# Reordering TensorE's step in a graph-attention kernel: projections put between the weighings

## The chip, the cores and the metric

The kernel runs on one core of a Trainium2 chip. The metric is the device time of one execution in microseconds (us). Engines are named as in the profile: PE is TensorE, PEld its loading of the stationary operand, DVE is VectorE, ACT is ScalarE, POOL is GpSimd, SP is the engine that issues the DMAs.

## The reference

The kernel computes a residual block around one graph-attention layer, for x of shape (8, 1024, 64) and an integer matrix adj of shape (8, 1024, 1024) that is 1 in about 1 of 128 places and 0 elsewhere. There are 8 heads of 64 columns.

```
h = max(layernorm(x), 0)
q, k, v = h@Wq+bq, h@Wk+bk, h@Wv+bv              # split into 8 heads
s = leaky_relu(q.k/8 + edge_bias[adj], 0.2)      # s is -1e9 where adj == 0
out = softmax(s) @ v                             # per head
result = x + (out as 512 columns) @ Wp + bp
```

## The kernel before

Rows are taken in groups of 16 query rows times 8 heads, which fill 128 partitions. Since few keys are set in adj for 16 rows, each group gathers at most 32 keys out of every 128 by a product with a matrix of zeros and ones (onehot), 256 slots for all 1024 keys. A tile is 128 rows, 8 groups; a pair is two groups; so a graph is 8 tiles or 32 pairs, and the kernel has 64 tiles or 256 pairs. Keys and values are never projected: the scores are taken against the gathered normed rows, and what is weighed is projected afterwards, head by head, with the products of Wv and Wp (w_ext).

All engines run the same count of steps s, one per pair, and each has its own function step(b, s) that issues what is due, in the order in which it is written there. Constants give the lag of each stage (line 43 to 45): a stage with lag L works on pair s - L, and a stage that is due once a tile has its work in every fourth step. Nothing else orders the work; engines meet in semaphores. Steps are told apart here by s modulo 4, as step 0, 1, 2 and 3. One graph is 32 steps; after a ramp of 32 steps the main loop has a body of 64 steps (two graphs) that is run three times, and the last two graphs are written out.

What TensorE does in a step, with the letters used further on, and its line:

- S, scores (L1174, L1175): four products with 256 columns streamed, into row_bank. Waits for VectorE's take of the scores before.
- T, turn_y (L1185): four transposes of the masked scores w, into turned_bank. Waits for VectorE's Y of the step before.
- W, weigh (L1232): four fp32 products of the exponentials pt with the gathered rows nat_sb. In the records each fp32 product is two loads and two matmuls, so eight of each.
- G and M, gather_keys (L1197) and gather_masks (L1209): two products each.
- N, natural (L1220): four products that turn the gathered keys back.
- A, turn_adj (L1240): eight bf16 transposes of adj, in step 1. C, count (L1248): eight small products, in step 2. P, project (L1263): four fp32 products (one head each, eight loads and eight matmuls), half a tile's heads in step 3 (lag 27) and the other half in step 0 (lag 28). These three share the PSUM bank adj_bank, and each waits until the one before has been read: P's by VectorE's norm, A's by ScalarE's copy_adj, C's by VectorE's take_counts.
- R, rank (L1255), in step 0; the making of the queries, Q (L1322), in steps 1 and 3; and four rarer products (L1308, L1331, L1339). They share q_bank (the program's misc) in the same way.

Before the change a step's order on TensorE is S T W G M N A C P R and then the rest of q_bank. ScalarE follows in that order: exp (L1456), copy_o (L1464), copy_keys (L1447), copy_masks (L1438), copy_natural (L1473), copy_adj (L1430), and the queries' high parts (L1483).

VectorE's order is Y (L1701, the leaky relu of two groups), take_counts (L1629), take_scores (L1678, two groups), flag_used (L1637), norm (L1762 to L1777: one half of a tile's heads is divided by its sums; the first half, e = 0, also has L1764 and L1773, and waits until GpSimd has summed the tile before), low_q (L1652, two instructions), take_ranks (L1645), small work on the row maxima (L1735, L1742, L1752), mark (L1690, onehot), pick_beta (L1662, L1666).

GpSimd's is line (L1039, two), convert (L1016, step 0, it makes adj_bf), add_heads (L1027 three times and L1030: it sums a tile's heads and adds x), and the adding of a constant to x_res twice a graph.

Of the kernel before, what the change touches and what calls it, by code (L numbers as in the profile page):

```python
# [20 lines left out]
def preln_graph_attention(nc, x, adj, Wq, bq, Wk, bk, Wv, bv, edge_bias, Wp, bp, out):  # L21
# [4 lines left out]
    B, M, D = x.shape  # L26
# [15 lines left out]

    LOAD, CONV, TURN_A, COUNT, USED, RANK, VAL, ONEHOT = 0, 4, 5, 6, 7, 8, 9, 9
    MASK, MASK_OUT, TFILL, QFILL, BETA, COLSUM, VEC = 10, 14, 13, 9, 6, 18, 22
    SCORE, A_LINE, Y, TURN, PV, X_ADD, PROJ, NORM, SUM, OUT = 17, 19, 20, 21, 22, 24, 27, 28, 30, 31
    K0, SETTLED = 32, 24
# [6 lines left out]
    with ExitStack() as ctx, ExitStack() as prep, ExitStack() as fast:  # L53
# [230 lines left out]
        def tile(b, s, lag):  # L284
            return every(b, s, lag, 4)
# [794 lines left out]
        def _(pe):  # L1080
# [44 lines left out]
            def adj_bank_uses(b, s):  # L1125
                t = tile(b, s, TURN_A)
                if t is not None:
                    yield adj_copied, TPG * b + t + 1
                t = tile(b, s, COUNT)
                if t is not None:  # L1130
                    yield cnt_ready, TPG * b + t + 1
                due = piece(b, s, PROJ, 2)
                if due is not None:
                    yield proj_taken, 2 * (TPG * b + due[0]) + due[1] + 1
# [88 lines left out]

            def weigh(b, p):
                n, t = PPG * b + p, p // 4
                pe.wait_ge(probs_ready, n + 1)
                pe.wait_ge(nat_copied, n + 1)
                if later(n):
                    pe.wait_ge(o_copied, n)
                for u in range(2):  # L1230
                    for k in range(2):
                        last = pe.matmul(o_part[0:D + 1, P * u:P * u + P], nat_sb[:, t % 2, p % 4 * 2 + u, k, :],  # L1232
                                         pt[:, p % 2, u, k, :], start=(k == 0), stop=(k == 1))
                last.then_inc(pv_done, 1)

# [21 lines left out]

            def project(b, t, e, s):
                n = TPG * b + t
                pe.wait_ge(o_copied, 4 * n + 4)  # L1260
                free(adj_bank_uses, b, s, len(list(adj_bank_uses(b, s))) - 1)
                for h in range(4):
                    last = pe.matmul(adj_bank[:, (D + 1) * h:(D + 1) * h + D + 1], ot_sb[0:D + 1, t % 2, 4 * e + h, :],  # L1263
                                     w_ext[0:D + 1, 4 * e + h, :], start=True, stop=True)
                last.then_inc(proj_done, 1)

            def step(b, s):
                p = pair(b, s, SCORE)
                if p is not None:
                    scores(b, p)  # L1270
                p = pair(b, s, TURN)
                if p is not None:
                    turn_y(b, p)
                p = pair(b, s, PV)
                if p is not None:
                    weigh(b, p)
                due = piece(b, s, TFILL, 4)
# [6 lines left out]
                if p is not None:  # L1284
                    natural(b, p)
                t = tile(b, s, TURN_A)
                if t is not None:
                    turn_adj(b, t, s)
                t = tile(b, s, COUNT)
                if t is not None:  # L1290
                    count(b, t, s)
                due = piece(b, s, PROJ, 2)
                if due is not None:
                    project(b, *due, s)
                i = 0
# [69 lines left out]
        def _(act):  # L1365
# [121 lines left out]
            def step(b, s):  # L1487
                p = pair(b, s, TURN)
                if p is not None:
                    exp(b, p)  # L1490
                p = pair(b, s, PV)
                if p is not None:
                    copy_o(b, p)
                due = piece(b, s, TFILL, 4)
                if due is not None:
                    copy_keys(b, *due)
                due = piece(b, s, MASK, 4)
                if due is not None:
                    copy_masks(b, *due)
                p = pair(b, s, SCORE)  # L1500
                if p is not None:
                    copy_natural(b, p)
                t = tile(b, s, TURN_A)
                if t is not None:
                    copy_adj(b, t)
                due = q_piece(b, s, QFILL)
                if due is not None:
                    high_q(b, *due)
                g = every(b, s, COLSUM, PPG)
                if g is not None:  # L1510
                    act.wait_ge(col_sums, b + g + 1)
                    nc.scalar.activation(mean_rep[:, :], misc[:, 0:1].to_broadcast([P, P]), ACT.Copy, scale=1.0 / M)\
                        .then_inc(mean_ready, 1)
                g = every(b, s, VEC, PPG)
                if g is not None:
                    act.wait_ge(vec_done, b + g + 1)
                    nc.scalar.activation(vecs[:, bass.ds(D * (b + g), D)], misc[:, 0:D], ACT.Copy).then_inc(vec_ready, 1)
# [30 lines left out]
        def _(dve):  # L1548
# [109 lines left out]
            def pick_beta(b, g, half):  # L1658
# [4 lines left out]
                                               head_rows[:, :], same_q[:, :].unsqueeze(1).to_broadcast([P, CAP, GQ]),  # L1663
                                               ALU.add, ALU.mult).then_inc(beta_picked, 1)
                dve.wait_ge(beta_picked, 2 * n + half + 1)
                nc.vector.tensor_reduce(beta[:, bass.ds(2 * PPG * b + 2 * PPG * g + CAP * half, CAP)],  # L1666
# [28 lines left out]
            def step(b, s):  # L1695
# [8 lines left out]
                if t is not None:  # L1704
                    take_counts(b, t)
                p = pair(b, s, SCORE)
                if p is not None:
# [3 lines left out]
                if t is not None:  # L1711
                    flag_used(b, t)
                    if t % TPG == TPG - 1:

                        dve.wait_ge(adj_copied, TPG * b + t + 1)
                        cols = square_sums_adj[:, bass.ds(TPG * b + t - TPG + 1, TPG)]
                        nc.vector.tensor_tensor(cols, cols, cnt_sums[:, :], ALU.subtract).then_inc(kinds_noted, 1)
                due = piece(b, s, NORM, 2)
                if due is not None:
                    norm(b, *due)  # L1720
                due = q_piece(b, s, QFILL + 1)
                if due is not None:
                    low_q(b, *due)
                t = tile(b, s, VAL)
                if t is not None:
                    take_ranks(b, t)
                four = p is not None and p % 2 == 1
# [12 lines left out]
                if four:  # L1740
                    dve.wait_ge(neg_ready, n + 1)
                    nc.vector.scalar_tensor_tensor(shift[:, cols], wmax[:, cols], -1.0, shift_neg[:, cols],  # L1742
                                                   ALU.mult, ALU.min).then_inc(shift_ready, 1)
                if t is not None and t % TPG == TPG - 1:
                    dve.wait_ge(val_ready, TPG * b + t + 1)
                    nc.vector.tensor_tensor(val_top[:, :], val_top[:, :], val_max[:, :], ALU.max).then_inc(vals_noted, 1)
                due = beta_piece(b, s, BETA + 1)
                if due is not None:
                    pick_beta(b, *due)
                if four:  # L1750
# [106 lines left out]
```

## Time and profile before

| | |
|---|---|
| time, median of 3 runs | 1049.67 us (1048.76 to 1053.98) |
| the profiled execution's own time | 1053.46 us |
| its span, first to last instruction | 1051.7 us |
| PE, PEld busy | 989.4 us (94%), 974.2 us (93%) |
| DVE busy | 917.3 us (87%) |
| ACT, POOL busy | 779.8 us (74%), 493.6 us (47%) |
| mean granted TensorE clock | 0.985 |

A record's duration on PE contains the pipeline's depth, so durations of neighbours overlap; the time from one start to the next tells what an instruction costs there. The same holds for DVE: neighbours overlap by some 0.08 us.

### The profile page before, as it was taken

How to read it: one execution, taken by the hardware profiler on the slowest of the kernel's cores; microseconds unless marked ns; L12 is line 12 of the kernel's file. 1: busy time of each engine (PE TensorE's matmuls, PEld its weight loads, DVE VectorE, ACT ScalarE, POOL GpSimd, SP SyncE). 2: the span in 40 equal slices, each digit the busy share in tenths (PEclk: the TensorE clock that was granted, in tenths of full speed). 3: DMA queues.
4: the chain of work that ended last, by engine and by line, in shares of the span. 5: the costliest groups of instructions: out<-in, count | busy, mean ns of one | idle time of the engine just before them, and what ended most of it. 6: DMA issues, size and time to landing. Idle time of an engine off the chain costs nothing.

```text
span 1051.7 us, 32494 instructions
## 1 busy us (share of the span) xinstructions
PE 989.4 (94%) x9056; PEld 974.2 (93%) x9056; DVE 917.3 (87%) x3409; ACT 779.8 (74%) x1737; POOL 493.6 (47%) x865
## 2 busy tenths in 40 slices
PE   5568999999999999999999999999999999999995
PEld 4458999999999989999999999999999999999995
DVE  4958899889998989989999869989998999989984
ACT  3567887788778877787777757788878877878762
POOL 1003444554455445554554434455455544545454
PEclk9998999999999999999999979999999999999998
DMA  7574434434344434434343433434434353534220
GB/s 171 177 223 121 115 113 133 116 107 139 110 132 115 115 116 117 125 105 139 114 135 104 123 95 113 133 96 125 133 107 146 86 149 101 142 106 120 70 75 9
DMA packets 190794, 125.52 MB, mean 119 GB/s; under 512 B 32832, under 2 KB 180300, under 8 KB 190604
## 3 DMA queue, kind: packets, MB, share of 16 engines
q1 hardware_dynamic: 189812, 122.75, 40.7%
q8 instruction: 83, 1.36, 0.5%
q14 instruction: 107, 0.88, 0.3%
q10 hardware_dynamic: 792, 0.53, 0.2%
HBM read 79.19 MB, written 44.04 MB: 117 GB/s over the span
## 4 chain that ended last, share of the span: by engine, by line
PE 64%; DVE 21%; issue 8%; ACT 2%; DMA 1%; DVEq 1%; POOL 1%; ACTq 0%; SPq 0%; POOLq 0%
PE bank L1232 14%; PE bank L1263 8%; PE bank L1185 7%; PE bank L1322 6%; PE bank L1220 6%; PE bank L1174 5%; DVE w L1678 5%; PE bank L1175 4%; PE bank L1209 4%; PE bank L1197 4%; PE bank L1240 3%; DVE onehot L1690 3%; DVE q_lo L1652 2%; DVE w L1701 2%; DVE o_all L1777 2%
## 5 line engine op out<-in xcount | busy, mean ns | idle before, releaser
L1039 POOL TENSOR_SCALAR a_line<-w,a_bias 128x256 f32<-128x256 f32 x512 | 261.8, 511 | 459.8 <-DVE w L1701 416.0
L1232 PE MATMUL bank<-pt,nat_sb 128*65 128x128 f32 x2048 | 267.2, 274 | 0.2
L1678 DVE CUSTOM_DVE_ANT_0 w<-bank,mask_rows 128x256 f32<-128x256 f32 x512 | 195.7, 419 | 60.2 <-PE bank L1175 41.4
L1456 ACT ACTIVATE pt<-bank 128x512 f32<-128x512 f32 x256 | 153.8, 601 | 118.0 <-PE bank L1185 113.6
L1701 DVE SCALAR_TENSOR_TENSOR w<-w,shift,a_line 128x256 f32<-128x256 f32 x512 | 231.2, 491 | 7.1 <-issue 4.6
L1232 PEld LDWEIGHTS bank<-pt,nat_sb 128*65 128x65 f32 x2048 | 232.4, 139 | 0.6 <-issue 0.6
L1690 DVE TENSOR_TENSOR onehot<-val,counts_to 128x512 fp32r<-128x512 f32 x256 | 176.5, 689 | 9.8 <-DVE val_max L1645 9.2
L1438 ACT ACTIVATE mask_own<-bank,mask_bias 128x512 bf16<-128x512 f32 x256 | 174.8, 683 | 1.4 <-PE bank L1209 1.4
L1185 PE MATMUL bank<-ident,w 128*128 128x128 f32 x1024 | 154.9, 274 | 0.0
L1447 ACT ACTIVATE t_sb<-bank 128x512 fp32r<-128x512 f32 x256 | 150.1, 586 | 3.2 <-PE bank L1197 3.0
L1174 PE MATMUL bank<-t_sb,q_hi 128*128 128x256 f32 x512 | 144.3, 303 | 5.8 <-issue 4.7
L1263 PE MATMUL bank<-w_ext,ot_sb 65*128 65x65 f32 x1024 | 139.8, 280 | 5.0 <-DVE o_all L1777 4.5
L1464 ACT ACTIVATE ot_sb<-bank 65x256 f32<-65x256 f32 x256 | 97.7, 382 | 56.9 <-PE bank L1232 56.9
L1483 ACT ACTIVATE q_hi<-bank,q_bias 128x256 fp32r<-128x256 f32 x256 | 107.4, 474 | 42.0 <-PE bank L1322 42.0
L1220 PEld LDWEIGHTS bank<-both_halves,t_sb 128*128 128x128 f32 x1024 | 137.6, 192 | 0.0
L1220 PE MATMUL bank<-both_halves,t_sb 128*128 128x64 f32 x1024 | 136.8, 257 | 0.0
L1027 POOL TENSOR_TENSOR o_all<-o_all 128x256 f32<-128x256 f32 (+2 forms) x192 | 126.4, 659 | 21.3 <-DVE o_all L1777 6.3
L1175 PE MATMUL bank<-t_sb,q_lo 128*128 128x256 f32 x512 | 134.6, 285 | 0.0
L1263 PEld LDWEIGHTS bank<-w_ext,ot_sb 65*128 65x128 f32 x1024 | 125.4, 193 | 5.9 <-DVE o_all L1777 2.5
L1197 PE MATMUL bank<-onehot,h_nl 128*128 128x256 f32 x512 | 124.7, 325 | 0.8 <-DVE onehot L1690 0.8
L1652 DVE SCALAR_TENSOR_TENSOR q_lo<-bank,q_bias,q_hi 128x256 fp32r<-128x256 f32 x256 | 111.4, 476 | 13.8 <-ACT q_hi L1483 9.1
L1185 PEld LDWEIGHTS bank<-ident,w 128*128 128x128 f32 x1024 | 119.6, 142 | 0.1
(135 smaller groups left out, 1634.3 us busy)
## 6 DMA issues: line engine op xcount, KB each, us to landing
adj_in<-in_adj_dram SPq DMA_DIRECT2D x64, 512.0 KB, 4.0
mask_store<-mask_own SPq DMA_DIRECT2D x64, 512.0 KB, 3.3
mask_rows<-mask_store SPq DMA_DIRECT2D x512, 64.0 KB, 2.4
nl_store<-nl_ring SPq DMA_DIRECT2D x7, 512.0 KB, 4.2
stack_store<-stage SPq DMA_DIRECT2D x7, 512.0 KB, 3.1
h_stack<-stack_store SPq DMA_DIRECT2D x7, 512.0 KB, 5.1
h_nl<-nl_store SPq DMA_DIRECT2D x28, 128.0 KB, 3.6
x_res<-in_x_dram SPq DMA_DIRECT2D x16, 128.0 KB, 2.2
```

The lines of the kernel that those rows point to most:

```text
L1039: nc.gpsimd.tensor_scalar(a_line[:, i % 2, :], w[:, i, :], 5.0, a_bias[:, i:i + 1], ALU.mult, ALU.add)\
L1174: pe.matmul(dst, q_hi[:, y % 2, GPT * (t % 2) + g, :], keys, start=True, stop=False)
L1175: last = pe.matmul(dst, q_lo[:, y % 2, GPT * (t % 2) + g, :], keys, start=False, stop=True)
L1185: last = pe.transpose(turned_bank[:, P * (2 * u + k):P * (2 * u + k) + P], w[:, slot(p, u), P * k:P * k + P], ident[:, :])
L1197: last = pe.matmul(t_bank[:, 256 * i:256 * i + 256], h_nl[:, 2 * f + i, :], onehot[:, t % 2, 2 * f + i].rearrange("p g j -> p (g j)"), sta ...
L1220: last = pe.matmul(nat_bank[:, D * (2 * u + k):D * (2 * u + k) + D], keys[:, P * k:P * k + P], both_halves[:, :], start=True, stop=True)
L1232: last = pe.matmul(o_part[0:D + 1, P * u:P * u + P], nat_sb[:, t % 2, p % 4 * 2 + u, k, :], pt[:, p % 2, u, k, :], start=(k == 0), stop=(k ...
L1263: last = pe.matmul(adj_bank[:, (D + 1) * h:(D + 1) * h + D + 1], ot_sb[0:D + 1, t % 2, 4 * e + h, :], w_ext[0:D + 1, 4 * e + h, :], start= ...
L1438: nc.scalar.activation(mask_own[:, t % 2].rearrange("p g t j -> p t g j")[:, 2 * f:2 * f + 2], m_bank[:, :].rearrange("p (t g j) -> p t g ...
L1678: nc.vector.tensor_tensor_reduce(w[:, i, :], row_bank[:, SLOTS * u:SLOTS * u + SLOTS], mask_rows[:, t % 2, p % 4 * 2 + u, :], 0.25, LEAST_ ...
L1690: nc.vector.tensor_tensor(onehot[:, t % 2, 2 * f:2 * f + 2].rearrange("p t g j -> p (t g) j"), val[:, t % 2, cols * f:cols * f + cols].uns ...
L1701: nc.vector.scalar_tensor_tensor(w[:, i, :], w[:, i, :], shift[:, i:i + 1], a_line[:, i % 2, :], ALU.add, ALU.max).then_inc(y_ready, 1)
```

## The change

It edits the order in which each engine's step issues its work, and lags.

- TensorE: S G M N T W A C R and the rest of q_bank. P is no longer a block of its own: weigh takes the projection that is due and issues one head's product behind each of its four. P's two halves come at lags 28 and 30, steps 0 and 2, so that A (step 1) and C (now lag 7, step 3) each stand alone in their step. weigh waits, in addition, for adj_bank to be free when a projection is due. In steps that have no pair left to weigh (behind the last graph) P is issued alone, as before.
- ScalarE: keys, masks, natural, exp, copy_o, adj, queries.
- VectorE: flag_used (now lag 8, step 0), take_ranks (step 1 still) and the first half of pick_beta are placed before take_scores. The second half (keep_beta) stays at the end. norm comes at lags 29 and 31, steps 1 and 3; take_counts comes in step 0.
- GpSimd and SP: add_heads at lag 32 for 30 (step 0 for 2), the store of the output at 33 for 31.

```diff
-    LOAD, CONV, TURN_A, COUNT, USED, RANK, VAL, ONEHOT = 0, 4, 5, 6, 7, 8, 9, 9
+    LOAD, CONV, TURN_A, COUNT, USED, RANK, VAL, ONEHOT = 0, 4, 5, 7, 8, 8, 9, 9
-    SCORE, A_LINE, Y, TURN, PV, X_ADD, PROJ, NORM, SUM, OUT = 17, 19, 20, 21, 22, 24, 27, 28, 30, 31
+    SCORE, A_LINE, Y, TURN, PV, X_ADD, PROJ, NORM, SUM, OUT = 17, 19, 20, 21, 22, 24, 28, 29, 32, 33
...
-            def weigh(b, p):
+            def weigh(b, p, due, s):
                 n, t = PPG * b + p, p // 4
                 pe.wait_ge(probs_ready, n + 1)
                 pe.wait_ge(nat_copied, n + 1)
                 if later(n):
                     pe.wait_ge(o_copied, n)
+                if due is not None:
+                    free(adj_bank_uses, b, s, len(list(adj_bank_uses(b, s))) - 1)
                 for u in range(2):
                     for k in range(2):
                         last = pe.matmul(o_part[0:D + 1, P * u:P * u + P], nat_sb[:, t % 2, p % 4 * 2 + u, k, :],
                                          pt[:, p % 2, u, k, :], start=(k == 0), stop=(k == 1))
-                last.then_inc(pv_done, 1)
+                        if (u, k) == (1, 1):
+                            last.then_inc(pv_done, 1)
+                        if due is not None:
+                            project(b, *due, 2 * u + k)
...
-            def project(b, t, e, s):
-                n = TPG * b + t
-                pe.wait_ge(o_copied, 4 * n + 4)
+            def wait_projection(b, t, e, s):
+                pe.wait_ge(o_copied, 4 * (TPG * b + t) + 4)
                 free(adj_bank_uses, b, s, len(list(adj_bank_uses(b, s))) - 1)
-                for h in range(4):
-                    last = pe.matmul(adj_bank[:, (D + 1) * h:(D + 1) * h + D + 1], ot_sb[0:D + 1, t % 2, 4 * e + h, :],
-                                     w_ext[0:D + 1, 4 * e + h, :], start=True, stop=True)
-                last.then_inc(proj_done, 1)
+
+            def project(b, t, e, h):
+                last = pe.matmul(adj_bank[:, (D + 1) * h:(D + 1) * h + D + 1], ot_sb[0:D + 1, t % 2, 4 * e + h, :],
+                                 w_ext[0:D + 1, 4 * e + h, :], start=True, stop=True)
+                if h == 3:
+                    last.then_inc(proj_done, 1)
...
 # TensorE's step: turn_y and weigh from behind scores to behind natural
+                p = pair(b, s, TURN)
+                if p is not None:
+                    turn_y(b, p)
+                p, due = pair(b, s, PV), piece(b, s, PROJ, 2, 2)
+                if p is not None:
+                    weigh(b, p, due, s)
+                elif due is not None:
+                    wait_projection(b, *due, s)
+                    for h in range(4):
+                        project(b, *due, h)
...
 # ScalarE's step: exp and copy_o from its head to behind copy_natural
...
 # VectorE's step, ahead of take_scores
+                t = tile(b, s, USED)
+                if t is not None:
+                    flag_used(b, t)
+                t = tile(b, s, VAL)
+                if t is not None:
+                    take_ranks(b, t)
+                due = beta_piece(b, s, BETA + 1)
+                if due is not None:
+                    pick_beta(b, *due)
...
-                due = piece(b, s, NORM, 2)
+                due = piece(b, s, NORM, 2, 2)
```

## Rows read from the trace of the kernel before

**Rows 1.** The page's chain of work that ended last, by engine.

```profile
PE 64%; DVE 21%; issue 8%; ACT 2%; DMA 1%; DVEq 1%; POOL 1%; ACTq 0%; SPq 0%; POOLq 0%
```

**Rows 2.** Stretches: us, busy us (x instructions) of PE, PEld, DVE, ACT, POOL; clock, DMA.

```profile
600.00:720.00 120.00, 116.00 (x1041) 114.75 (x1039) 102.60 (x387) 88.55 (x198) 57.47 (x100) 0.94 0.40 115
...
840.00:960.00 120.00, 119.04 (x1125) 118.19 (x1123) 110.59 (x422) 94.85 (x213) 61.53 (x108) 1.00 0.43 123
```

**Rows 3.** Waits of PEld: waited for, us in total, times, longest us.

```profile
PEld bank L1240 <- DVE o_all L1777: 10.2, 34, 0.6
```

**Rows 4.** PE in time, one tile's R and one eight tiles later: start us, us.

```profile
756.00 0.19 PE L1255 MATMUL bank<-used,lower 128*128 128x64 bf16 x1
...
875.02 0.20 PE L1255 MATMUL bank<-used,lower 128*128 128x64 bf16 x1
```

**Rows 5.** PE in time: a step 2, the P of a step 0, the A of step 1.

```profile
865.33 1.04 PE L1232 MATMUL bank<-pt,nat_sb 128*65 128x128 f32 x8
866.12 0.48 PE L1197 MATMUL bank<-onehot,h_nl 128*128 128x256 f32 x2
...
866.68 0.53 PE L1220 MATMUL bank<-both_halves,t_sb 128*128 128x64 f32 x4
867.04 0.36 PE L1248 MATMUL bank<-groups,adj_bf 128*128 128x8 bf16 x8
...
874.11 1.08 PE L1263 MATMUL bank<-w_ext,ot_sb 65*128 65x65 f32 x8
...
877.39 0.53 PE L1220 MATMUL bank<-both_halves,t_sb 128*128 128x64 f32 x4
878.05 0.61 PE L1240 MATMUL bank<-ident_bf,adj_bf 128*128 128x128 bf16 x8
```

**Rows 6.** Weight loads by form: names, shapes, count | busy us, mean ns | idle before.

```profile
L1232 PEld LDWEIGHTS bank<-pt,nat_sb 128*65 128x65 f32 x2048 | 232.4, 139 | 0.6 <-issue 0.6
...
L1263 PEld LDWEIGHTS bank<-w_ext,ot_sb 65*128 65x128 f32 x1024 | 125.4, 193 | 5.9 <-DVE o_all L1777 2.5 <-issue 1.8 <-ACT ot_sb L1464 1.5
L1185 PEld LDWEIGHTS bank<-ident,w 128*128 128x128 f32 x1024 | 119.6, 142 | 0.1
```

**Rows 7.** DVE in time, step 0 and the head of step 1.

```profile
872.20 0.42 DVE L1678 CUSTOM_DVE_ANT_0 w<-bank,mask_rows 128x256 f32<-128x256 f32 x1 [0.70 <-issue]
...
872.89 0.16 DVE L1762 TENSOR_SCALAR den<-bank 128x4 f32<-128x4 f32 x1
...
873.88 0.86 DVE L1652 SCALAR_TENSOR_TENSOR q_lo<-bank,q_bias,q_hi 128x256 fp32r<-128x256 f32 x2
874.66 0.15 DVE L1735 SCALAR_TENSOR_TENSOR shift_neg<-wmax,beta 128x4 f32<-128x4 f32 x1
...
875.60 0.87 DVE L1701 SCALAR_TENSOR_TENSOR w<-w,shift,a_line 128x256 f32<-128x256 f32 x2
```

**Rows 8.** DVE in time, step 1: the second half's norm, the ranks, onehot.

```profile
877.08 0.16 DVE L1762 TENSOR_SCALAR den<-bank 128x4 f32<-128x4 f32 x1
...
877.82 0.21 DVE L1645 CUSTOM_DVE_ANT_0 val<-bank,used 128x64 f32<-128x64 f32 x1
...
878.08 0.69 DVE L1690 TENSOR_TENSOR onehot<-val,counts_to 128x512 fp32r<-128x512 f32 x1
```

**Rows 9.** POOL in time: two lines and a convert; add_heads of another tile.

```profile
865.96 2.02 POOL L1027 TENSOR_TENSOR o_all<-o_all 128x256 f32<-128x256 f32 x3
868.06 0.32 POOL L1030 TENSOR_TENSOR x_res<-x_res,o_all 128x64 f32<-128x64 f32 x1
...
871.30 1.13 POOL L1039 TENSOR_SCALAR a_line<-w,a_bias 128x256 f32<-128x256 f32 x2 [1.31 <-DVE w L1701]
872.51 1.05 POOL L1016 TENSOR_SCALAR adj_bf<-adj_in 128x1024 bf16<-128x1024 int32 x1
```

**Rows 10.** PE in time at the main loop's second turning back.

```profile
612.19 0.57 PE L1174 MATMUL bank<-t_sb,q_hi 128*128 128x256 f32 x1 [2.36 <-issue]
```

**Rows 11.** DVE in time: the last tile's first norm, behind the last scores.

```profile
1041.94 0.16 DVE L1762 TENSOR_SCALAR den<-bank 128x4 f32<-128x4 f32 x1 [2.23 <-POOL x_res L1030]
```

More of the change, by code:

```diff
@@ L1131, in adj_bank_uses @@
                     yield cnt_ready, TPG * b + t + 1
-                due = piece(b, s, PROJ, 2)
+                due = piece(b, s, PROJ, 2, 2)
                 if due is not None:
@@ L1270, in step @@
                     scores(b, p)
[L1271 to L1276, printed above, removed]
                 due = piece(b, s, TFILL, 4)
@@ L1291, in step @@
                     count(b, t, s)
-                due = piece(b, s, PROJ, 2)
-                if due is not None:
-                    project(b, *due, s)
                 i = 0
@@ L1487, in step @@
             def step(b, s):
[L1488 to L1493, printed above, removed]
                 due = piece(b, s, TFILL, 4)
@@ L1502, in step @@
                     copy_natural(b, p)
+                p = pair(b, s, TURN)
+                if p is not None:
+                    exp(b, p)
+                p = pair(b, s, PV)
+                if p is not None:
+                    copy_o(b, p)
                 t = tile(b, s, TURN_A)
@@ L1664, in pick_beta, with keep_beta @@
                                                ALU.add, ALU.mult).then_inc(beta_picked, 1)
+            def keep_beta(b, g, half):
+                n = b + g
                 dve.wait_ge(beta_picked, 2 * n + half + 1)
@@ L1711, in step @@
                 if t is not None:
-                    flag_used(b, t)
                     if t % TPG == TPG - 1:
@@ L1723, in step @@
                     low_q(b, *due)
-                t = tile(b, s, VAL)
-                if t is not None:
-                    take_ranks(b, t)
                 four = p is not None and p % 2 == 1
@@ L1743, in step @@
                                                    ALU.mult, ALU.min).then_inc(shift_ready, 1)
+                t = tile(b, s, VAL)
                 if t is not None and t % TPG == TPG - 1:
@@ L1748, in step @@
                 if due is not None:
-                    pick_beta(b, *due)
+                    keep_beta(b, *due)
                 if four:
```

## The prediction

> **What bounds the kernel now.** I read the chain of waits first, then the busy time by stretch, the waits of the weight loads, and last TensorE's and VectorE's records in time. The chain lies on PE for 64% and on DVE for 21% [rows 1]. In an undisturbed stretch of 120 us PE is busy for 119.0 and DVE for 110.6 [rows 2]: PE sets the pace, and DVE has 9.4 us in 120 to spare, 1.2 us of a tile. Eight tiles take 875.02 - 756.00 = 119.02 us, 14.88 a tile [rows 4]. PE's only regular wait is A for VectorE's norm, some 0.30 us (10.2 us in 34 waits [rows 3]; in the rows 878.05 - 877.39 = 0.66 where the same four products before C take 867.04 - 866.68 = 0.36 [rows 5]). So PE's own sum is near 14.55 a tile.
>
> **How PE's time is made up.** The weighing's eight matmuls start 0.109 us apart (866.12 - 865.33 = 0.79: seven intervals and the 0.028 in which the next record begins early), the projection's eight 0.114 (875.02 - 874.11 = 0.91) [rows 4, 5], though the weighing streams 128 columns twice over and the projection only 65. The loads differ the other way: 65 columns are recorded with 139 ns, 128 columns with 193 [rows 6]. Both are explained if a load runs beside the matmul before it, and an interval is the larger of two things, the next load and the present stream: a weighing is held by its stream (0.109), a projection by its load (0.11). The 65-column load is then 0.11 - (0.193 - 0.139) = 0.057, and by its record of 142 ns the transposes' load is 0.06 [rows 6]. The projection's stream, 65 columns for the weighing's 128, is 0.055.
>
> The Trainium skill (TensorE: Matmul & The Clock Gate, section Packing small matmuls) says a load overlaps running matmuls only when the row groups differ. The rows speak against it: with 0.057 of load behind 0.107 of stream a weighing would take 0.164, and takes 0.109. By that rule interleaving could win nothing; it is a rival below.
>
> **The change on PE, by intervals.**
> - In a step with a projection, before: S to T 0.118, W to G 0.111, N to P 0.111, seven W intervals 0.763, seven P intervals 0.78: 1.88. After: S to G 0.118, N to T 0.06, and inside, four W to W (0.109), four W to P (0.111), four P to P (0.111), three P to W (0.057, the larger of 0.057 and 0.055): 1.50. Together 1.67, which is 0.21 less, twice a tile.
> - In a step with A or C, before S to T, W to G and N to A make 0.118 + 0.111 + 0.027; after, S to G, N to T and W to A make 0.118 + 0.06 + 0.109: 0.03 more, twice a tile.
> - Sum 2 x 0.21 - 2 x 0.03 = 0.37 us a tile less. PE's sum falls from 14.55 to 14.18. If the transposes' load were a full 0.111, N to T would be 0.05 longer in four steps, and 0.17 would be left.
> I take 0.37, because the record of 142 ns lies at the short load.
>
> **VectorE.** Nothing is added to its work (13.7 us a tile). Its parts, start to start: Y 0.79 (0.87 less the 0.08 by which neighbours overlap), take 0.69, norm of the first half 0.99, low_q 0.78, the rest with onehot 0.94 in a step 0 [rows 7]; norm of the second half 0.74, ranks 0.26 [rows 8]. Counts have the ranks' shape, some 0.2; flag_used is some 0.13. By step, before: 4.2, 3.1, 3.2, 2.5; after: step 0 loses the norm and gains counts and flag, 3.5; step 1 has the long norm for the short, 3.3; step 2 stays; step 3 gains 0.74 and loses 0.33, 2.9. That is more even, and PE's steps become 3.4 to 3.6 (before 2.9 to 4.2).
>
> What counts is A's wait. From S of step 0 to A of step 1 VectorE's chain changes by -0.99 + 0.33 (moved in step 0) + 0.25 (long for short norm) + 0.26 (ranks now ahead of the take), -0.15, and PE's by -0.21 + 0.03 = -0.18: nearly the same, so the wait of 0.30 stays. But VectorE reaches step 0 later: step 3 costs it 0.41 more, PE 0.67 less. The 0.70 for which it idled ahead of that take [rows 7] covers all but 0.38. So A's wait grows by 0 to 0.38, or goes with its 0.30 if the evener steps let VectorE catch up. In step 2 low_q waits for ScalarE's queries, which stand behind A and copy_adj in the same order as before. I take 0.10, nearest to no change, because the spare 1.2 us of VectorE exceed what PE saves. Net 0.27 a tile; both ends -0.01 and 0.67.
>
> **The other edits.** ScalarE is idle for a fifth of the stretch [rows 2] and follows PE's new order: every copy comes behind the product it reads, and copies of one step are wanted a step later; nothing. copy_o of step 2 now waits for the projection woven in, 0.17 us, wanted a step later; nothing. pick_beta ahead of the take comes twice a graph, 16 times: it reads q_bank sooner, so that Q of step 3 need not wait for the end of VectorE's step, and it delays that take. Each is at most one instruction over 512 columns, as long as onehot's 0.69 [rows 8], so 11 us either way at the worst; the two stand against each other in one step, and I take 0. The second half of the new wait in weigh is for adj_bank: in step 0 for counts, read at the head of VectorE's step, in step 2 for copy_adj, issued over 2 us earlier; nothing, and if it were late, all behind W on PE (A or C, R, Q, the next S) would be late with it. SP's stores come two steps later with no reader.
>
> Tail: behind the last scores P of the last tiles comes every second step rather than in two neighbouring steps. The last first-half norm already waits for GpSimd's sum of the tile before (2.23 us [rows 11]); that sum now begins one step of PE and VectorE later, which has little in it there, some 1.3 us (a P block of 0.9 and a hand-over). Bounds 0 and 3. The ramp is unchanged.
>
> **Sum.** 63 tiles x 0.27 = 17.0, less 1.3: 15.7 us. The profiled execution took 1053.46 (span 1051.7 and 1.8 around it): it becomes 1037.8. Between 600 and 720 us its mean granted clock is 0.94 [rows 2], so a part of that stretch ran at 1.2 instead of 2.4 GHz; just before it PE stood still for 2.36 us at the loop's turning back [rows 10]. It lies 3.8 above the median, and the change leaves that place as it is. From the median: 1049.7 - 15.7 = 1034.0.
>
> **Rivals.**
> - GpSimd eats it. The first half's norm waits until add_heads has summed the tile before. That was two steps apart; now add_heads is in step 0 and the norm in step 1. In step 0 GpSimd does two lines (1.13), convert (1.05, with gaps 1.2) and add_heads (868.38 - 865.96 = 2.4) [rows 9]. The lines start 0.4 behind the start of Y, so it ends 0.4 + 1.2 + 1.2 + 2.5 = 5.3 us behind it. The norm is due at 3.5 + 0.79 + 0.26 + 0.69 = 5.2, later where VectorE waits for S. The two are even. If add_heads comes 0.25 later, the gain of 0.27 is gone: 1049.7 + 1.3 = 1051.
> - It comes out slower by the same place: if add_heads is stretched by 0.5 (its three sums vary; half a microsecond is a fifth of it), A and all behind it wait 0.5 longer in each tile, against 0.27 gained: + 63 x 0.23 + 1.3 = 15.8, 1065.5. It decides from 0.25 of lateness on. Against it: the norm has VectorE's waits as cover.
> - VectorE catches up and A's wait goes: 63 x 0.67 - 1.3 = 41, 1009. For it speak the evener steps; against it that then VectorE, at 13.7 of 14.2, would hardly ever wait.
> - Loads don't overlap across the two kinds of product (the skill's rule, or a pair of fp32 matmuls that doesn't take the next load early): an interval P to W stays 0.11, 2 x 3 x 0.053 = 0.32 a tile are not won; of 0.37 less 0.10 that leaves -0.05, a loss of 3: 1054 with the tail.
>
> **How the numbers follow.** Forecast 0.52, with its own range 1026 to 1042. A's wait gone, below 1026: 0.14. GpSimd just eats it: 0.15. Slower by it: 0.12. No overlap: 0.07. What this kernel's measurement can tell from no change is 0.5%, 5.2 us. Faster: 0.52 + 0.14 and a part of the third: 0.69. Same: 0.17. Slower: 0.14. The range 1018 to 1054 leaves out 0.07 below and 0.12 above.
>
> **What would show it.** In the profile after: the interval from the first woven weighing to the next product in steps 0 and 2, 1.50 us for 16 matmuls (1.8 if loads don't overlap); N to T under 0.1; R to R over eight tiles near 116.9 us; A's load waiting 0.3 to 0.5 us for o_all; add_heads ending just ahead of the norm of step 1, with no wait of L1762 for GpSimd in the body. The prediction is wrong if that last wait appears in most tiles, or if A's wait is above 0.6.

## The result, and the profile after

| | before | after |
|---|---|---|
| median (range), 5 runs each on one chip | 1049.70 us (1048.76 to 1058.36) | 1064.31 us (1059.74 to 1065.69) |
| ratio, 95% interval | | 1.0102 [1.0062, 1.0143] |
| profiled execution, its span | 1053.46, 1051.7 us | 1059.74, 1058.0 us |
| mean granted TensorE clock | 0.985 | 0.986 |
| R to R over eight tiles | 119.02 us [rows 4] | 120.72 us |

The kernel became slower by about 1%, where 1034 was forecast. The changed kernel's profiled execution is its shortest one, so the difference of the two profiled times, 6.3 us, is less than that of the medians. The period agrees with the medians: 1.7 to 1.8 us in eight tiles, times 63/8, is 13.4 to 14.2.

The page of the changed kernel, its busy times and the chain that ended last by engine (before: [rows 1]):

```profile
PE 967.7 (91%) x9056; PEld 944.8 (89%) x9056; DVE 943.2 (89%) x3409; ACT 784.0 (74%) x1737; POOL 488.3 (46%) x865
...
PE 48%; DVE 32%; issue 12%; DMA 2%; ACT 2%; DVEq 2%; POOL 1%; SPq 1%; ACTq 0%; POOLq 0%
```

PE's busy time fell by 22 us and DVE's rose by 26, though DVE was given no work. A third of the chain now lies on DVE. The undisturbed stretch shows the same (before, in [rows 2]: PE 119.04, DVE 110.59):

```profile
840.00:960.00 120.00, 114.71 (x1106) 112.72 (x1106) 112.94 (x414) 93.76 (x209) 60.65 (x106) 1.00 0.41 119
```

PE lacks 5.3 us in 120. The waits of the weight loads say where (before: 10.2 us in 34 waits, at most 0.6 [rows 3]), and those of DVE say that the norm (L1780) was held by GpSimd's sum only twice:

```profile
PEld bank L1247 <- DVE o_all L1795: 41.6, 46, 1.5
```

```profile
DVE den L1780 <- PE bank L1270: 5.9, 3, 2.4
...
DVE den L1780 <- POOL x_res L1030: 2.9, 2, 2.2
```

PE in time: the R eight tiles earlier, then N, T, the woven W and P and the R of a step 0, and the end of the step 1 behind it (for [rows 4, 5]):

```profile
757.94 0.19 PE L1262 MATMUL bank<-used,lower 128*128 128x64 bf16 x1
...
876.24 0.53 PE L1220 MATMUL bank<-both_halves,t_sb 128*128 128x64 f32 x4
876.60 0.65 PE L1185 MATMUL bank<-ident,w 128*128 128x128 f32 x4
877.09 0.38 PE L1236 MATMUL bank<-pt,nat_sb 128*65 128x128 f32 x2
877.31 0.33 PE L1270 MATMUL bank<-w_ext,ot_sb 65*128 65x65 f32 x2
877.48 0.38 PE L1236 MATMUL bank<-pt,nat_sb 128*65 128x128 f32 x2
...
878.66 0.19 PE L1262 MATMUL bank<-used,lower 128*128 128x64 bf16 x1
...
880.58 1.04 PE L1236 MATMUL bank<-pt,nat_sb 128*65 128x128 f32 x8
882.30 0.61 PE L1247 MATMUL bank<-ident_bf,adj_bf 128*128 128x128 bf16 x8 [0.68 <-DVE o_all L1795]
```

From the first woven product to R behind the block takes 878.66 - 877.09 = 1.57 us. A starts 1.72 behind W; its eight matmuls take 0.76 and the step to A 0.109, so A waited 0.85. DVE in time, one line of the step 2 before and then that step 0, and POOL in time in the same step 0 show why the norm is late:

```profile
871.43 0.16 DVE L1759 SCALAR_TENSOR_TENSOR shift<-wmax,shift_neg 128x4 f32<-128x4 f32 x1
...
878.38 0.68 DVE L1702 TENSOR_TENSOR onehot<-val,counts_to 128x512 fp32r<-128x512 f32 x1
878.98 0.42 DVE L1759 SCALAR_TENSOR_TENSOR shift<-wmax,shift_neg 128x4 f32<-128x4 f32 x1
879.43 0.17 DVE L1770 TENSOR_TENSOR a_bias<-shift,beta 128x4 f32<-128x4 f32 x1
879.51 1.02 DVE L1713 SCALAR_TENSOR_TENSOR w<-w,shift,a_line 128x256 f32<-128x256 f32 x2
```

```profile
876.54 1.05 POOL L1016 TENSOR_SCALAR adj_bf<-adj_in 128x1024 bf16<-128x1024 int32 x1
877.55 2.24 POOL L1027 TENSOR_TENSOR o_all<-o_all 128x256 f32<-128x256 f32 x3
879.86 0.39 POOL L1030 TENSOR_TENSOR x_res<-x_res,o_all 128x64 f32<-128x64 f32 x1
```

The shift works on four numbers a partition, and takes 0.42 us here; in the step 2 before (871.43) the same instruction took 0.16. The timeline merges the three adds into one row. Taken singly, the second of them runs from 878.36 to 879.38: it took 1.02 us, where its form (128x128) takes 0.47 in the mean in a_double34 below. It overlaps onehot first; then the shift, which starts at 878.98, ends at 879.40, just behind it.

### The profile page after: what moved, and what is told of

It reads as the page before. It is cut to its first block, busy times and chain, and to the rows that moved or that the text cites. A ratio compares the mean times of both kernels' runs of the same rounds, so it can differ in the third digit from the quotient of the medians.

```text
span 1058.0 us, 32512 instructions
## 1 busy us (share of the span) xinstructions
PE 967.7 (91%) x9056; PEld 944.8 (89%) x9056; DVE 943.2 (89%) x3409; ACT 784.0 (74%) x1737; POOL 488.3 (46%) x865
## 4 chain that ended last, share of the span: by engine, by line
PE 48%; DVE 32%; issue 12%; DMA 2%; ACT 2%; DVEq 2%; POOL 1%; SPq 1%; ACTq 0%; POOLq 0%
PE bank L1236 10%; DVE w L1690 7%; PE bank L1185 5%; DVE onehot L1702 5%; PE bank L1331 5%; PE bank L1270 4%; PE bank L1174 4%; PE bank L1220 4%; DVE w L1713 4%; PE bank L1175 4%; PE bank L1247 3%; DVE q_lo L1661 3%; PE bank L1209 3%; PE bank L1197 3%; DVE shift L1759 2%
## 5 line engine op out<-in xcount | busy, mean ns | idle before, releaser
L1039 POOL TENSOR_SCALAR a_line<-w,a_bias 128x256 f32<-128x256 f32 x512 | 258.3, 505 | 473.8 <-DVE w L1713 430.1
L1236 PE MATMUL bank<-pt,nat_sb 128*65 128x128 f32 x2048 | 329.7, 274 | 1.1 <-ACT ot_sb L1473 0.8
L1236 PEld LDWEIGHTS bank<-pt,nat_sb 128*65 128x65 f32 x2048 | 224.5, 139 | 1.9 <-issue 1.8
L1702 DVE TENSOR_TENSOR onehot<-val,counts_to 128x512 fp32r<-128x512 f32 x256 | 185.4, 724 | 0.5
L1270 PE MATMUL bank<-w_ext,ot_sb 65*128 65x65 f32 x1024 | 172.4, 252 | 2.7 <-DVE o_all L1795 2.7
L1185 PE MATMUL bank<-ident,w 128*128 128x128 f32 x1024 | 167.7, 287 | 0.3 <-ACT pt L1465 0.3
L1270 PEld LDWEIGHTS bank<-w_ext,ot_sb 65*128 65x128 f32 x1024 | 156.3, 194 | 3.0 <-issue 3.0
L1465 ACT ACTIVATE pt<-bank 128x512 f32<-128x512 f32 x256 | 158.2, 618 | 1.0 <-PE bank L1185 0.3
L1027 POOL TENSOR_TENSOR o_all<-o_all 128x256 f32<-128x256 f32 (+2 forms) x192 | 125.7, 655 | 19.2 <-DVE o_all L1795 8.8
L1174 PEld LDWEIGHTS bank<-t_sb,q_hi 128*128 128x128 f32 x512 | 98.0, 191 | 11.7 <-issue 6.2
L1439 ACT ACTIVATE adj_t<-bank 128x1024 fp32r<-128x1024 bf16 x64 | 65.7, 1027 | 57.2 <-PE bank L1247 57.0
```

The costliest lines, as they stand in the source:

```text
L1039: nc.gpsimd.tensor_scalar(a_line[:, i % 2, :], w[:, i, :], 5.0, a_bias[:, i:i + 1], ALU.mult, ALU.add)\
L1174: pe.matmul(dst, q_hi[:, y % 2, GPT * (t % 2) + g, :], keys, start=True, stop=False)
L1185: last = pe.transpose(turned_bank[:, P * (2 * u + k):P * (2 * u + k) + P], w[:, slot(p, u), P * k:P * k + P], ident[:, :])
L1465: nc.scalar.activation(pt[:, p % 2], turned_bank[:, :].rearrange("p (u k r) -> p u k r", u=2, k=2), ACT.Exp, scale=0.8).then_inc(probs_rea ...
L1702: nc.vector.tensor_tensor(onehot[:, t % 2, 2 * f:2 * f + 2].rearrange("p t g j -> p (t g) j"), val[:, t % 2, cols * f:cols * f + cols].uns ...
```

## The experiments

All were timed in 3 rounds. Two columns come from the single records of a trace between 240 and 960 us. "Lengthened" is what a VectorE record takes over the lower quartile of its form in the same run, where that is more than 0.02 us, summed by step. "To A" is the mean time from the last W (where N is last, from N) to A; unhindered it is 0.109 (from N 0.116, as from N to C, which hardly ever waits). The kernel before ran in each batch: 1050.95 in the first, 1052.23, 1052.75.

| kernel | median (range), us | ratio [95%] | eight tiles, us | lengthened in steps 0, 1 / 2, 3, us | to A, us |
|---|---|---|---|---|---|
| before | 1049.70 | | 119.0 | 7.4 / 18.2 | 0.397 (N) |
| after | 1064.31 | 1.0102 [1.0062, 1.0143] | 120.8 | 40.7 / 0 | 0.906 |
| a_double34 | 1035.09 (1033.73 to 1037.01) | 0.984 [0.9811, 0.9869] | 116.8 | 8.3 / 9.8 | 0.407 |
| b_double32 | 1074.70 (1072.73 to 1076.59) | 1.0216 [1.0182, 1.025] | 123.1 | 19.6 / 0.4 (29.7 / 0.4, see below) | 0.598 (N) |
| a_block | 1069.86 (1065.71 to 1070.35) | 1.0165 [1.0129, 1.0201] | 121.7 | 39.9 / 0 | 0.733 |
| a_swap | 1060.31 (1059.04 to 1062.42) | 1.0091 [1.0061, 1.0122] | 120.1 | 37.8 / 0 | 0.844 |
| a_double32 | 1060.06 (1057.98 to 1065.17) | 1.008 [1.0047, 1.0114] | 120.7 | 39.9 / 0 | 0.901 |
| a_memset32 | 1037.07 (1035.90 to 1041.11) | 0.9833 [0.9797, 0.9869] | 116.5 | 5.3 / 2.6 | 0.424 |
| a_double34_block | 1044.01 (1041.09 to 1045.24) | 0.9906 [0.987, 0.9943] | 118.1 | 7.9 / 9.8 | 0.304 |
| a_best | 1041.83 (1036.88 to 1042.57) | 0.987 [0.9825, 0.9915] | 117.5 | 1.2 / 20.8 | 0.303 |
| b_order | 1051.31 (1049.08 to 1055.26) | 0.9983 [0.9957, 1.001] | 119.1 | 7.8 / 18.9 | 0.324 |
| a_sum31 | 1093.77 (1092.97 to 1094.55) | 1.0383 [1.0344, 1.0421] | 124.9 | 64.6 / 2.3 | 0.933 |
| a_double34_swap | 1040.88 (1038.97 to 1043.18) | 0.989 [0.985, 0.993] | 117.5 | 6.8 / 15.0 | 0.390 |
| a_double34_ranks | 1038.66 (1037.46 to 1038.77) | 0.9862 [0.9826, 0.9898] | 117.1 | 8.9 / 18.9 | 0.325 |

Names with a_ are edits of the changed kernel, those with b_ of the one before.

**a_double34: add_heads back into step 2.** With the sum two steps later the norm would wait for it, so o_all gets two buffers, by tile.

```diff
-    ... NORM, SUM, OUT = ... 29, 32, 33
+    ... NORM, SUM, OUT = ... 29, 34, 35
-        o_all = sb("o_all", [P, H, D], F32, fast)
+        o_all = sb("o_all", [P, 2, H, D], F32, fast)
-                if e == 0 and later(n):
-                    dve.wait_ge(summed, n)
+                if e == 0 and later(n, 2):
+                    dve.wait_ge(summed, n - 1)
# and o_all[:, t % 2, ...] in norm and add_heads; the output's store is at 35 for 33
```

> The changed kernel with o_all in two buffers and add_heads at lag 34 (step 2, as before the change) instead of 32 (step 0). Theory 1 (place of add_heads): in step 0 its three sums stand beside VectorE's instructions with two SBUF inputs (onehot, shift, Y), which become longer there, in the stretch that A of step 1 waits for. Then those stretched instructions go back to steps 2 and 3, A's wait falls from some 0.8 us to 0.4, eight tiles from 120.8 to about 117 us, and the time to 1036 (1030 to 1042). Theory 2 (order in the norm): A's wait comes from the long first-half norm and the ranks now ahead of it; then add_heads' place is worth little: 1055 to 1064.

It took 1035.09, as the first theory said. Its stretch and A's wait:

```profile
840.00:960.00 120.00, 118.35 (x1147) 116.78 (x1146) 112.47 (x428) 96.85 (x217) 62.40 (x109) 1.00 0.43 123
```

```profile
PEld bank L1248 <- DVE o_all L1796: 16.0, 27, 1.1
```

The whole loss lies in where add_heads is placed. Two things changed, though, the place and the wait; the next ones part them.

**b_double32: the same move, made alone on the kernel before**, with the same two buffers (SUM 30 to 32, from step 2 to step 0).

> The kernel before with o_all in two buffers and add_heads at lag 32 (step 0) instead of 30 (step 2): only the place of add_heads is that of the change. Theory 1: VectorE's chain to A grows by some 0.4 to 0.6 us a tile, 1075 (1065 to 1085). Theory 2: within 5 us of before, 1050.

It took 24 us more than the kernel before, 1074.70 as expected, with no edit to TensorE's order. There the norm stands in step 0 itself: the mean of its x_res (L1774) goes from 360 to 643 ns, and A and P both wait for it.

```profile
L1774 DVE SCALAR_TENSOR_TENSOR x_res<-vecs,alone,x_res 128x64 f32<-128x64 f32 x64 | 41.1, 643 | 1.0 <-issue 0.2
```

```profile
PEld bank L1241 <- DVE o_all L1778: 20.3, 41, 0.9
PEld bank L1264 <- DVE o_all L1778: 12.5, 36, 0.6
```

The table's measure fails here: x_res is lengthened in most tiles, so that its lower quartile in this run is itself 0.52 us, where it is 0.26 in the kernel before. Against the forms of the kernel before, steps 0 and 1 have 29.7 us (7.4 before) and all steps 30.1 (25.6 before). The sum grew by 4.5 us in these 48 tiles, the part ahead of A by 22, and the time by 24 us in 64 tiles: it is the place that counts, ahead of A.

**a_block: the change without the weaving**; P is a block behind W.

```diff
                         if (u, k) == (1, 1):
                             last.then_inc(pv_done, 1)
-                        if due is not None:
-                            project(b, *due, 2 * u + k)
...
-                    weigh(b, p, due, s)
-                elif due is not None:
+                    weigh(b, p, None, s)
+                if due is not None:
```

> The changed kernel with the four products of a projection issued as one block behind the weighing again. Theory 1 and 2: the interleaving does what was worked out (a load of 65 columns behind a projection's stream), so that TensorE gets 2 x 3 x 0.05 = 0.3 us more a tile; since VectorE is what A waits for, about half of it shows, 1064 + 10 (1066 to 1082). Rival (the interleaving itself costs): faster than the changed kernel, 1050 or less.

1069.86, inside the range expected. Without the weaving eight tiles take 0.9 us more, and the medians differ by 5.5 us. The two ratios' intervals overlap, so that by the times alone a gain from weaving isn't shown in the slower kernel; nothing speaks for a loss.

**a_swap: in the first half's norm, o_all ahead of x_res.**

```diff
                 if e == 0:
...
-                    nc.vector.scalar_tensor_tensor(x_res[...], vecs[...], alone[:, :], ...)
                 nc.vector.tensor_tensor(o_all[:, heads, :], parts[:, :, 0:D], ...)
+                if e == 0:
+                    nc.vector.scalar_tensor_tensor(x_res[...], vecs[...], alone[:, :], ...)
```

> The changed kernel with the addition to x_res in the first-half norm put behind the writing of o_all, so that A is released 0.26 to 0.4 us sooner. Theory 2: all of that shows, 1064 - 19 = 1045. Theory 1: VectorE's total is the same and its stretched instructions remain; half of it shows, 1050 to 1058.

A miss: 1060.31 is above what either theory gave. The 0.3 us taken out from ahead of A left "to A" at 0.844, only 0.06 less.

**a_double32: the norm's wait for the sum taken away, and nothing moved** (the two buffers of a_double34 with SUM left at 32).

> The changed kernel with o_all in two buffers, add_heads left at lag 32 (step 0). It takes away only the wait of the first-half norm for the sum of the tile before. Theory (add_heads beside VectorE's instructions with two SBUF inputs): no change against the changed kernel, 1058 to 1066, A's wait still 0.7 to 0.8 us. Rival (the prediction's own: the norm waits for the sum): 1040 or less.

1060.06, eight tiles 120.7 for 120.8: the period stays where it was, and the ratios' intervals, [1.0047, 1.0114] and [1.0062, 1.0143], overlap. The wait that my two rivals rested on costs nothing that these runs can tell.

**a_memset32: the same GpSimd time in the same place, without reading.** The three adds become fills of 704 zeros a partition in a tile of their own, so the sum over heads is left out of the result.

```diff
-                    nc.gpsimd.tensor_tensor(o_all[:, 0:heads, :], o_all[:, 0:heads, :], o_all[:, heads:2 * heads, :], ALU.add)\
+                    pool.nop(nofuse=True)
+                    nc.gpsimd.memset(scratch[:, :], 0.0)\
...
# and scratch = sb("scratch", [P, 704], F32, fast)
```

> The changed kernel with the three sums of add_heads replaced by three fills of a scratch tile with 704 zeros a partition, about as long (some 0.7 us each) but reading nothing; the sum over heads is left out, only the first head is added to x. Theory (the shared read of SBUF is what VectorE waits for): onehot, shift and Y in step 0 go back to their undisturbed lengths (683, 155, 480 ns), A's wait to 0.3 to 0.4, 1036 to 1044. Rival (GpSimd's time or place as such, whatever it does): no change, 1060 or more.

1037.07, though GpSimd is busy in that place as long as before (131.8 us of fills for 125.7 us of adds). By form, of a_memset32:

```profile
L1704 DVE TENSOR_TENSOR onehot<-val,counts_to 128x512 fp32r<-128x512 f32 x256 | 178.3, 697 | 0.5
...
L1761 DVE SCALAR_TENSOR_TENSOR shift<-wmax,shift_neg 128x4 f32<-128x4 f32 x128 | 19.9, 156 | 0.1
...
L1029 POOL MEMSET scratch<- 128x704 f32 x192 | 131.8, 686 | 24.4 <-DVE o_all L1797 8.7 <-POOL scratch L1029 0.4
```

and of the changed kernel:

```profile
L1713 DVE SCALAR_TENSOR_TENSOR w<-w,shift,a_line 128x256 f32<-128x256 f32 x512 | 234.7, 498 | 6.1 <-issue 5.2 <-POOL a_line L1039 0.8
L1702 DVE TENSOR_TENSOR onehot<-val,counts_to 128x512 fp32r<-128x512 f32 x256 | 185.4, 724 | 0.5
L1759 DVE SCALAR_TENSOR_TENSOR shift<-wmax,shift_neg 128x4 f32<-128x4 f32 x128 | 43.0, 336 | 0.1
...
L1027 POOL TENSOR_TENSOR o_all<-o_all 128x256 f32<-128x256 f32 x64 | 61.0, 953 | 9.2 <-DVE o_all L1795 8.8
```

In the record of one such step (the three fills stand in one row again):

```profile
876.23 0.68 DVE L1704 TENSOR_TENSOR onehot<-val,counts_to 128x512 fp32r<-128x512 f32 x1
876.24 2.29 POOL L1029 MEMSET scratch<- 128x704 f32 x3
...
876.83 0.15 DVE L1761 SCALAR_TENSOR_TENSOR shift<-wmax,shift_neg 128x4 f32<-128x4 f32 x1
...
877.10 0.87 DVE L1715 SCALAR_TENSOR_TENSOR w<-w,shift,a_line 128x256 f32<-128x256 f32 x2
```

Taken singly, the first fill ends at 876.92, under the shift; the second runs from 877.04 to 877.73, and the first Y lies wholly inside it, from 877.10 to 877.57, and takes its shortest time, 0.48. That holds throughout the stretch from 240 to 960 us: beside fills the shift takes 0.154 to 0.163 (17 records) and Y 0.476 to 0.486 (86); beside the adds of the changed kernel the shift takes 0.41 to 0.70 (47) and Y 0.66 to 0.69 (23, beside an add alone). low_q, which has one of its inputs in PSUM, takes 0.466 to 0.481 beside these same adds (38), and 0.472 to 0.485 elsewhere.

So it is neither GpSimd's time nor its lateness, but that it reads SBUF while VectorE runs an instruction with two SBUF inputs.

**a_double34_block: is the weaving worth its price with add_heads out of the way?** Both edits together.

> a_double34 (o_all in two buffers, add_heads at lag 34) with the projections as blocks behind the weighing. With the disturbance gone TensorE sets the pace, so the interleaving should be worth nearly all of its 0.3 us a tile: 1035 + 15 (1046 to 1056). If VectorE set the pace there too, it would be worth half or less: 1037 to 1045.

A miss: 1044.01, in the range of the rival (half or less), and under the 1046 to 1056 that I held likelier. Against 1035.09 weaving gives 9 us, 0.14 a tile, of the 0.30 that it gives on PE: from S to S, steps 2 and 0 take 3.61 and 3.55 us in the median for 3.46 and 3.40. A part goes back, since A waits less where PE is slower (0.304 for 0.407).

**b_order: only TensorE's and ScalarE's order**, T and W behind N, on the kernel before.

```diff
 # TensorE's step; the same for exp and copy_o in ScalarE's
-                p = pair(b, s, TURN)
-                if p is not None:
-                    turn_y(b, p)
-                p = pair(b, s, PV)
-                if p is not None:
-                    weigh(b, p)
...
 # and these lines again behind natural
```

> The kernel before with only the order of TensorE and ScalarE changed (turns and weighing behind the gathers; projections as blocks, old lags, add_heads in step 2). By the intervals this saves 2 x 0.054 in the steps with a projection and costs 2 x 0.028 in those with A or C, 0.05 us a tile: 1050 - 3, so 1043 to 1051. Rival (the turns' place is bad for the exchange with VectorE or ScalarE): 1055 or more.

1051.31, just above the 1043 to 1051 expected, and no difference from the kernel before: the order alone is neither gain nor loss.

**a_best: a_double34, the swapped norm, and the constant's adding moved** (X_ADD 24 to 26).

> a_double34 with two more things taken out of the chain before A: the addition to x_res stands behind o_all's writing in the first-half norm, and the adding of the constant to x_res (GpSimd, twice a graph) is at lag 26 (step 2) for 24 (step 0), where it lengthened onehot and shift by 6.5 us in 720. A's wait is 0.19 us in the median and 0.3 in the mean there; if it goes, 1035 - 12 to - 18: 1017 to 1023. Rival (A's wait comes from other steps, those with pick_beta): 1030 or more.

A miss: 1041.83 is slower than a_double34. A waits less, C instead:

```profile
PEld bank L1256 <- DVE o_all L1793: 11.7, 21, 0.8
PEld bank L1248 <- DVE o_all L1793: 10.4, 18, 0.7
```

**a_double34_swap: of those two edits, only the norm's order.**

> a_double34 with the addition to x_res behind o_all in the first-half norm (the constant stays at lag 24). A's wait of 0.3 us in the mean should mostly go: 1035 - 6 to - 12, 1023 to 1029. a_best, which had this and the constant in step 2, took 1042: if the constant's new place was what cost it, this one is clearly below 1035; if the norm's new order was, this one is at 1040.

1040.88: the swap alone takes about what a_best took, 0.7 us more in eight tiles than a_double34, and the constant's place nothing that shows. The ratios' intervals of a_double34 and of this run overlap a little, so that the 6 us between the medians rest on the period too. Its lengthening goes from 9.8 to 15.0 us in steps 2 and 3, nearly all of it in step 2's shift_neg (1.6 to 7.9 us), and C waits for 6.5 us where it waited for 2.5.

**a_double34_ranks: take_ranks back behind the norm.**

```diff
-                t = tile(b, s, VAL)
-                if t is not None:
-                    take_ranks(b, t)
...
 # the same three lines behind low_q, as before the change
```

> a_double34 with take_ranks in its old place behind the norm. The ranks take 0.22 to 0.26 us ahead of the norm that A waits for; behind it they come later for Q, which stands behind A anyway. If they matter, 1035 - 5 to - 10; if A's wait is set elsewhere or the ranks then hold Q up, 1035 to 1042.

1038.66: "to A" is 0.08 shorter, and the time no better. Again what is won ahead of A is met by more lengthening in steps 2 and 3 (18.9), and C waits for 9.4 us where it waited for 2.5.

**a_sum31: add_heads one step earlier than in the change**, right behind the second half's norm (SUM 32 to 31).

> The changed kernel with add_heads at lag 31 (step 3) for 32, one buffer as it was: its sums follow the second-half norm at once and lie beside onehot of step 3 and Y of step 0, ahead of the stretch from S of step 0 to A. Shared read of SBUF: about the same lengthening in all, but half of it outside the stretch that A waits for: 1044 (1038 to 1052). If only the total lengthening counted, 1058 or more; if only that stretch counted, 1036.

The largest miss: 1093.77. GpSimd does its work in order, and the sum, now ahead of the lines and convert, makes these later too. Convert (1.05 us) then falls on VectorE's shift_neg, and the adds on Y:

```profile
909.24 1.05 POOL L1016 TENSOR_SCALAR adj_bf<-adj_in 128x1024 bf16<-128x1024 int32 x1
...
909.32 0.98 DVE L1752 SCALAR_TENSOR_TENSOR shift_neg<-wmax,beta 128x4 f32<-128x4 f32 x1
```

```profile
L1713 DVE SCALAR_TENSOR_TENSOR w<-w,shift,a_line 128x256 f32<-128x256 f32 x512 | 256.8, 542 | 7.9 <-issue 5.6 <-POOL a_line L1039 2.2
...
L1752 DVE SCALAR_TENSOR_TENSOR shift_neg<-wmax,beta 128x4 f32<-128x4 f32 x128 | 58.0, 453 | 0.1
```

In the changed kernel shift_neg takes 185 ns in the mean.

## Why the prediction was wrong

**The step that failed is "I take 0.10"**, the growth of A's wait: it measured 0.52 a tile. Its bounds, 0 to 0.38, counted VectorE's instructions at the durations that they had before. But VectorE's durations are not its own: where a two-input instruction meets a GpSimd instruction that reads SBUF, one of them stands still. The change moved add_heads, 2.4 us of such reads [rows 9], from step 2, where VectorE has time to spare, to step 0, whose work ends in the norm that A waits for. The sum names add_heads only as something that the norm could wait for.

**The size agrees.** Lengthening in steps 0 and 1 rose from 7.4 to 40.7 us between 240 and 960 us; over 48 tiles that is 0.69 a tile, enough for what A lost. Against a_double34, where A's wait is as good as before, "to A" is 0.50 longer (0.906 - 0.407), and a tile takes (120.8 - 116.8) / 8 = 0.50 longer: every part of A's delay is in the period. Against the kernel before, A's wait grew from 0.28 (0.397 - 0.116) to 0.80 (0.906 - 0.109), 0.52 a tile. The net is +0.22 a tile; so TensorE's own sum gave back 0.30.

**TensorE's intervals** came out near the sum, though not one by one. The 0.37 is 0.36 by its own terms, and 0.30 was gained. The 1.50 for a woven block adds up fifteen intervals, and those take 1.45; 1.57 is with the sixteenth, to R. N to W is 877.09 - 876.24 = 0.85, where the terms give 0.83, in four steps 0.08 less won. Taken singly, the last N to the first T is 0.111, above the 0.1 that was named as a sign. A cycle of two W and two P takes 0.39, as worked out, where the rival on row groups had 0.44, so nothing of that rival showed. But by the starts P to P takes 0.060 and P to W 0.110, where 0.111 and 0.057 were worked out: the rule "the larger of the next load and the present stream" gives the right sum, and not the right intervals. Why is not known.

**TensorE's steps**, from S to S, are 3.40, 3.46 and 3.52 us in the median for steps 0, 2 and 3, as forecast (3.4 to 3.6). Step 1 takes 4.54, for in it PE waits for the norm.

**With the failed step mended the time comes out, in part by luck.** a_double34 keeps all other edits: 1035.09 against the 1034.0 forecast, eight tiles 116.8 against 116.9, A's load waiting 16.0 us in 27 waits, 0.6 each as against the 0.3 to 0.5 forecast. It gains 0.28 a tile for the 0.27 forecast, but from 0.30 of intervals for 0.37, and 0.02 more of A's wait for 0.10: two misses that cancel. The edits priced at nothing (ScalarE's order, pick_beta, the new wait for adj_bank) show no price in this sum. From the last S to the last instruction that computes, the profiled runs take 19.6 us before, 22.2 in the changed kernel and 21.5 in a_double34, so that the tail grew by 2.6 and 1.9 where 1.3 was taken.

**The rivals.** "It comes out slower by the same place" gave 1065.5, near the 1064.31 measured, and is not what happened; that the two numbers agree is luck. Its mechanism, the norm waiting until add_heads has finished, shows in 2 waits with 2.9 us, and taking the wait away (a_double32) leaves the period as it was. Of the two signs I named for being wrong, the wait of L1762 (now L1780) for GpSimd did not appear, and A's wait above 0.6 did. "GpSimd eats it" fell with it. A's wait did not go either.

**What could have been read beforehand.** In the trace of the kernel before, by form, the shift takes 269 ns in the mean, and by turns some 0.40 us beside add_heads (step 2) and 0.15 with nothing in its way (step 0):

```profile
L1742 DVE SCALAR_TENSOR_TENSOR shift<-wmax,shift_neg 128x4 f32<-128x4 f32 x128 | 34.5, 269 | 0.1
```

These are instructions that add_heads met already, where it was harmless. The Trainium skill (SBUF — State Buffer, section SBUF: two separate sides) says that VectorE and GpSimd share one pair of ports, held by one instruction to its end, with the other standing still, and that VectorE's instructions with two SBUF inputs need it only against a GpSimd instruction that reads SBUF. This case's traces agree: 0.55 us in the mean for the shift beside adds and 0.156 beside fills, and the end of one at the end of the other. By that rule the change moves a collision ahead of A, and I did not weigh it.

**What stays open.** Why a swap of two instructions, or the ranks' place, brings back what it saves by collisions two steps on was followed only as far as the sums by form and the waits; which pairs meet was not traced one by one. Whether convert could be kept off shift_neg by another order on GpSimd was not tried. The fastest of the kernels that ran and give the whole result is a_double34, 0.984 [0.9811, 0.9869] of the kernel before.

## What to carry to other kernels

When a change moves a GpSimd instruction, write down which VectorE instructions will run beside it in its new place, and which engine waits for these; here the same instructions in another place were worth 29 us (1064.31 for 1035.09). A GpSimd busy time that stays the same hides the cost: it shows in VectorE's mean by form, above all in tiny two-input instructions. Compare it with the shortest records of the form, or with another run: where most records of a form are held up, as x_res in b_double32, its quartile is held up too. Rows that merge several records of a timeline don't tell which of them ran when. And a rival whose number comes out is not yet shown: here the number was right and the mechanism wrong, and one run without the wait told them apart.

## What the runs showed of the hardware

- An instruction on 128x4 numbers, 0.15 us alone, is held for as long as a GpSimd read lasts: shift_neg took 0.98 us beside convert (1.05 us), which has a single SBUF input. It works the other way as well: adds of 128x128 took 658 ns in the mean in the changed kernel and 466 in a_double34.
- GpSimd's fills, which only write, hold up none of these: 686 ns each, with onehot at 0.68 to 0.69 and the shift at 0.15 to 0.16 beside them.
- Weaving products with a short load among products with a long one saves time on TensorE: in blocks the intervals are 0.109 us (W: 65 columns loaded, 128 streamed) and 0.112 (P: 128 loaded, 65 streamed), 0.44 for two of each; woven, two of each take 0.39.
